# A transformer kernel on one core: late slices normalised on VectorE and split in two places on GpSimd; biases and first queries split on GpSimd in the prelude, and ScalarE issuing part of the first key loads

## The reference

```
x = x + attention_a(norm(x))   # 16 heads of 16; softmax over 2048 keys; the output weighs the row's own v
x = x + ffn(norm(x))           # relu(x Wfc)^2 Wproj, then 5 steps of a spiking neuron, mean spike count
x = x + attention_b(norm(x))   # 16 heads; softmax(k v^T * temperature), applied to q
x = x + ffn(norm(x))
```

## Time and profile before

| what | value |
|---|---|
| three runs, median (lowest to highest) | 2801.47 us (2797.8 to 2804.88) |
| the profiled execution: its time / its span | 2799.21 us / 2797.4 us |
| PE / PEld busy | 2383.7 us (85%) / 1044.3 us (37%) |
| DVE / ACT busy | 2509.2 us (90%) / 2545.7 us (91%) |
| POOL busy | 1301.6 us (47%) |
| L1033 and L1006, DVE maxima, 2048 of them | 1216 and 1219 ns each |
| L1214 and L1257, ACT exp, 2048 of them | 1120 and 1098 ns each |

### The profile page before, as it was taken

One profiled execution on the slowest core, in us unless ns is written; L12 is line 12 of the kernel. 1 busy time (PEld: TensorE's weight loads), 2 busy tenths in 40 slices (PEclk: granted clock), 3 DMA queues, 4 the chain that ended last, 5 costly groups with the idle time before them and its releaser, 6 DMA issues. The chain is left out here.

```text
span 2797.4 us, 43801 instructions
## 1 busy us (share of the span) xinstructions
PE 2383.7 (85%) x12438; PEld 1044.3 (37%) x12672; DVE 2509.2 (90%) x2590; ACT 2545.7 (91%) x4753; POOL 1301.6 (47%) x1913
## 2 busy tenths in 40 slices
PE   5688878877877787777788999999999999999997
PEld 2244444433433443343342333333333333333334
DVE  5898888899999999999988999999999989999994
ACT  2899898999999999999988999999999989999994
POOL 1246666655554554555452244444434434443445
PEclk8999999999999999999999999999999999999999
DMA  6521212143311111111111111111111111111110
GB/s 201 126 63 45 75 44 75 38 100 76 70 35 43 37 35 36 42 30 34 50 36 50 34 45 42 34 40 44 42 31 46 42 29 47 42 37 37 44 28 16
DMA packets 190988, 141.32 MB, mean 51 GB/s; under 512 B 92163, under 2 KB 177669, under 8 KB 190726
## 3 DMA queue, kind: packets, MB, share of 16 engines
q1 hardware_dynamic: 190726, 138.28, 18.6%
HBM read 92.04 MB, written 41.94 MB: 48 GB/s over the span
## 5 line engine op out<-in xcount | busy, mean ns | idle before, releaser
L1033 DVE TENSOR_REDUCE nmax<-score 128x1 f32<-128x1024 f32 x1024 | 1198.2, 1216 | 136.9 <-PE score L814 129.1
L1006 DVE TENSOR_REDUCE nmax<-score 128x1 f32<-128x1024 f32 x1024 | 1211.0, 1219 | 81.2 <-PE score L752 70.1
L1214 ACT ACTIVATE big<-score,nmax 128x1024 f32<-128x1024 f32 x1024 | 1138.4, 1120 | 83.1 <-DVE nmax L1006 77.2
L1257 ACT ACTIVATE score<-score,nmax 128x1024 f32<-128x1024 f32 x1024 | 1118.7, 1098 | 58.2 <-DVE nmax L1033 55.6
L814 PE MATMUL score<-big,shared 128*128 128x512 bf16 x1956 | 627.5, 404 | 250.9 <-ACT score L1257 216.2
L752 PE MATMUL score<-shared 128*128 128x512 bf16 x1906 | 576.6, 385 | 77.5 <-ACT big L1214 48.9
L733 PE MATMUL bank_g<-big,qw 128*32 128x512 f32 x4096 | 547.4, 608 | 1.0 <-ACT qcol L1242 1.0
L752 PEld LDWEIGHTS score<-shared 128*128 128x128 bf16 x2048 | 137.8, 97 | 609.8 <-ACT big L1214 568.3
L814 PEld LDWEIGHTS score<-big,shared 128*128 128x128 bf16 x2048 | 137.1, 99 | 541.9 <-ACT score L1257 449.1
L708 PEld LDWEIGHTS bank_f<-norms,w_fc_sb 128*128 128x128 f32 x2048 | 278.4, 191 | 75.6 <-ACT hid L1179 36.9
L708 PE MATMUL bank_f<-norms,w_fc_sb 128*128 128x128 f32 x2048 | 296.9, 278 | 10.7 <-ACT hid L1179 9.7
(11 more groups left out here) (141 smaller groups left out, 1671.8 us busy)
## 6 DMA issues: line engine op xcount, KB each, us to landing
shared<-q_parts SPq DMA_DIRECT2D x256, 64.0 KB, 2.4
shared<-kb_parts SPq DMA_DIRECT2D x256, 64.0 KB, 2.3
shared<-vb_parts SPq DMA_DIRECT2D x256, 64.0 KB, 2.3
big<-k_parts SPq DMA_DIRECT2D x48, 192.0 KB, 5.0
big<-k_parts SPq DMA_DIRECT2D x24, 256.0 KB, 7.5
kb_parts<-pieces SPq DMA_DIRECT2D x96, 64.0 KB, 1.6
vb_parts<-pieces SPq DMA_DIRECT2D x96, 64.0 KB, 1.6
shared<-in_x SPq DMA_DIRECT2D x32, 128.0 KB, 2.4
```

Source lines behind the costliest of these rows:

```text
L1006: v.tensor_reduce(nmax[:, par, c // NCH, c % NCH:c % NCH + 1], score_b(turn, c)[:, :], AX.X, ALU.max, negate=True).then_inc(max_b, 1)
L1033: v.tensor_reduce(nmax[:, par, c // NCH, c % NCH:c % NCH + 1], score_a(turn, c)[:, :], AX.X, ALU.max, negate=True).then_inc(max_a, 1)
L1214: a.activation(expo[:, c // NCH, (c % NCH) * CH:(c % NCH + 1) * CH], score_b(turn, c)[:, :], ACT.Exp, bias=nmax[:, par, c // NCH, c % NCH: ...
L1257: a.activation(s[:, :], s[:, :], ACT.Exp, bias=nmax[:, par, c // NCH, c % NCH:c % NCH + 1], accum_out=esum[:, par, c // NCH, c % NCH:c % N ...
```

## The change

In the late rows (iterations 3 to 10): `slice_norm` is cut in two. POOL keeps the 1/sqrt(var) (`slice_rstd`), now behind `split_kv`; DVE does the two normalising instructions (`slice_norm`, at c = 25, and slice 0's in the prelude). The slice's statistics move from c = 17, 19 to c = 14, 16. `step_split` is cut in two: `first_part` (cast, subtract) stands before POOL's second `normalise`, `other_parts` (cast, subtract) at the very end of POOL's iteration.

In the prelude: the biases and the queries of group 0 (j = 1) are split by POOL; DVE does its norms first and then splits 0, 2, 3, 4. SP stores in the order j = 0, 2, 1, 3, then issues `load_q(0, 0)`, then stores j = 4. The key loads become seven: heads 0-3 first half, heads 0-1 second half, heads 2-3 second half, then heads 4-5, 6-8, 9-11, 12-15 whole. ScalarE issues the first (8 DMAs) as soon as groups 0 and 1 are stored, and half of the second (4 DMAs) when all are.

```diff
-KEY_LOADS = [(0, 2), (2, 5), (5, 9), (9, 13), (13, 16)]
+KEY_LOADS = [(0, 4, 0, SEQ // 2), (0, 2, SEQ // 2, SEQ), (2, 4, SEQ // 2, SEQ), (4, 6, 0, SEQ), (6, 9, 0, SEQ), (9, 12, 0, SEQ),
+             (12, 16, 0, SEQ)]
+POOL_SPLIT, STORE_ORDER = 1, [0, 2, 1, 3]
...
+        def split_of(j):
+
+            if j == POOL_SPLIT:
+                return q_split, 4
+            return p_split, 4 * (j if j < POOL_SPLIT else j - 1) + 4
...
+            for j in STORE_ORDER:
+                g, m0 = EARLY[j]
+                if j == 2:
+                    sp.wait_ge(bias_split, 4)
+                    for a in range(PARTS):
+                        sp.dma_start(bias[a:a + 1, :], bias_parts[a]).then_inc(bias_loaded, 16)
                 store_group(g, j, k_parts if m0 else q_parts)
...
+            sp.wait_ge(qk_stored[1], 16 * PARTS)
+            load_q(sp, 0, 0)
+            store_group(NE - 1, len(EARLY) - 1, k_parts)
+            for u in range(2):
+                load_slice(u)
             for r in range(2):
                 sp.wait_ge(qk_stored[r], 16 * PARTS * ((len(EARLY) + 1 - r) // 2))
...
+            early_load(1, range(0, 4))
+            early_load(2)
+            store_v(0)
+            early_load(3)
+            early_load(4)
+            load_q(sp, 1, 1)
+            early_load(5)
+            early_load(6)
...
+            def slice_norm(u):
+                dve.wait_ge(s_rstd, 2 * u + 2)
+                need(dve, s_tr, u)
+                dve.wait_ge(s_aggr, SLS * u + SLS)
+                for s in range(SLS):
+                    last = v.tensor_scalar(s_n[:, s, :], s_x[:, u % 2, s, :], s_mv[:, s, 0:1], s_rs[:, s:s + 1],
+                                           ALU.subtract, ALU.mult)
+                last.then_inc(s_xn, 1)
+
             stats(0)
             norm(0)
             stats(1)
             norm(1)
-            split_bias()
             stats(2)
-            split(0)
             norm(2)
-            split(1)
+            scale_bias()
             stats(3)
             norm(3)
+            split(0)
             for j in range(2, len(EARLY)):
                 split(j)
             slice_stats(0)
             slice_aggr(0)
+            slice_norm(0)
...
                     if u is not None and u + 1 < NSL:
-                        if c == 17:
+                        if c == 14:
                             slice_stats(u + 1)
-                        if c == 19:
+                        if c == 16:
                             slice_aggr(u + 1)
+                        if c == 25:
+                            slice_norm(u + 1)
...
+            act.wait_ge(qk_stored[0], 16 * PARTS * 2)
+            load_keys(act, 0, *KEY_LOADS[0], early_keys[0])
             take_v(0)
+            for r in range(2):
+                act.wait_ge(qk_stored[r], 16 * PARTS * ((len(EARLY) + 1 - r) // 2))
+            load_keys(act, 0, *KEY_LOADS[1], early_keys[1], range(4, 8))
...
             for g in range(NE):
                 group_rstd(g)
...
+            split_bias()
+            split_queries(POOL_SPLIT)
...
                 if i2 is not None:
                     spikes(i2, i2, par, 2, 3)
+                if w is not None:
+                    first_part(w)
                 if i1 is not None:
                     normalise(i1, 0, ffn_mv, ffn_step, xn[:, :], xin[:, 1 - par, :], ffn_tr, i1).then_inc(ffn_xn, 1)
-                if w is not None:
-                    step_split(w)
...
                 if i3 is not None:
                     split_kv(i3)
+                if u is not None and u + 1 < NSL:
+                    slice_rstd(u + 1)
...
                     result(i2, i2, par, x2_stored[par], 8 * (i2 - par))
-                if u is not None and u + 1 < NSL:
-                    slice_norm(u + 1)
+                if w is not None:
+                    other_parts(w)
```

More of the change, by code:

```diff
@@ L198, in build @@
         prod = shared2[:, 0:BANK]
+        qres = shared2[:, 0:KC * GROUP].rearrange("p (m n) -> p m n", m=KC)
         qcol = sb("qcol", [P, 2, D])
@@ L299, in stand_alone, with load_q, load_keys @@
                 need(eng, s, n)
+        def split_of(j):
+            if j == POOL_SPLIT:
+                return q_split, 4
+            return p_split, 4 * (j if j < POOL_SPLIT else j - 1) + 4
+        def load_q(eng, i, par):
+            for n in range(8):
+                src = q_parts[Q_SLOTS[n], :, bass.ds(i * P, P)].rearrange("(h d) n -> d h n", d=DH)
+                eng.dma_start(qstack[n:P:8, par, :, :], src).then_inc(q_loaded[par], 16)
+        def load_keys(eng, b, h0, h1, m0, m1, done, copies=range(8)):
+            for n in copies:
+                src = k_parts[K_SLOTS[n], h0 * DH:h1 * DH, b * SEQ + m0:b * SEQ + m1].rearrange("(h d) m -> d h m", d=DH)
+                eng.dma_start(keys[n:P:8, b, h0:h1, m0:m1], src).then_inc(done, 16)
         def tile_at(it, lag):
@@ L429, in store_slice @@
                           .then_inc(s_stored, 16)
[L431 to L439, removed]
             load_x(0)
@@ L515, in phase_a @@
                         stand_alone(sp, (scores_a, CPT * i))
-                        load_q(i + 1, 1 - par)
+                        load_q(sp, i + 1, 1 - par)
                     stand_alone(sp, (att_opt, i - 1), (ffn_x1, i - 1))
@@ L807, in phase_a @@
                     if i is not None:
-                        for n, (h, _) in enumerate(KEY_LOADS):
-                            if isinstance(i, int) and i == 0 and c == h * NCH:
+                        for n, (h, _, m, _) in enumerate(KEY_LOADS):
+                            if isinstance(i, int) and i == 0 and c == h * NCH + m // CH:
                                 pe.wait_ge(early_keys[n], 128)
@@ L905, in split @@
             def split(j):
+                first = split_of(j)[1] - 4
                 dve.wait_ge(p_qkf, j + 1)
@@ L1102, in take @@
             def take(j, m0):
-                need(act, p_split, 4 * (j - 1))
+                if j >= 2:
+                    act.wait_ge(*split_of(j - 2))
                 for m in range(KC):
@@ L1325, in group_rstd, with split_queries, split_bias, slice_rstd @@
                 g_.tensor_tensor(prstd[:, g, :], pvar[:, g, :], power[:, 0:SUB], ALU.pow).then_inc(p_rstd, 1)
+            def split_queries(j):
+                stand_alone(pool, (p_qkf, j + 1))
+                part, whole = pparts[j % 2], pk[j % 2]
+                g_.tensor_scalar(part[:, 0, :, :], whole, 1.0, 0.0, ALU.mult, ALU.add).then_inc(q_split, 1)
+                pool.wait_ge(q_split, 1)
+                g_.tensor_tensor(qres, whole, part[:, 0, :, :], ALU.subtract).then_inc(q_split, 1)
+                stand_alone(pool, (q_split, 2))
+                g_.tensor_scalar(part[:, 1, :, :], qres, 1.0, 0.0, ALU.mult, ALU.add).then_inc(q_split, 1)
+                pool.wait_ge(q_split, 3)
+                g_.tensor_tensor(part[:, 2, :, :], qres, part[:, 1, :, :], ALU.subtract).then_inc(q_split, 1)
+            def split_bias():
+                stand_alone(pool, (w_in_loaded, 16 * N_PRELUDE_LOADS))
+                g_.tensor_scalar(bias_parts[0], row_bias, 1.0, 0.0, ALU.mult, ALU.add).then_inc(bias_split, 1)
+                pool.wait_ge(bias_split, 1)
+                g_.tensor_tensor(bias_res, row_bias, bias_parts[0], ALU.subtract).then_inc(bias_split, 1)
+                stand_alone(pool, (bias_split, 2))
+                g_.tensor_scalar(bias_parts[1], bias_res, 1.0, 0.0, ALU.mult, ALU.add).then_inc(bias_split, 1)
+                pool.wait_ge(bias_split, 3)
+                g_.tensor_tensor(bias_parts[2], bias_res, bias_parts[1], ALU.subtract).then_inc(bias_split, 1)
             for g in range(NE):
                 group_rstd(g)
-            def slice_norm(u):
+            split_bias()
+            split_queries(POOL_SPLIT)
+            def slice_rstd(u):
                 stand_alone(pool, (s_aggr, SLS * u + SLS))
@@ L1334, in slice_norm, with first_part @@
                 g_.tensor_tensor(s_rs, s_var, power[:, 0:SLS], ALU.pow).then_inc(s_rstd, 1)
[L1336 to L1342, removed]
+            def first_part(w):
                 if w < NE - 1:
@@ L1350, in step_split, with other_parts @@
                 g_.tensor_tensor(s_res, s_f, s_parts[:, 0, :, :], ALU.subtract).then_inc(s_split, 1)
+            def other_parts(w):
                 stand_alone(pool, (s_split, 4 * w + 2))
@@ L1354, in step_split @@
                 g_.tensor_tensor(s_parts[:, 2, :, :], s_res, s_parts[:, 1, :, :], ALU.subtract).then_inc(s_split, 1)
-            slice_norm(0)
+            slice_rstd(0)
             def normalise(n, which, got, step, dst, src, free, count):
```

38 lines of the change are left out of this document (9 added, 29 removed).

## The result

The changed kernel takes 2787.53 us (median of 7 runs, 2782.4 to 2793.73), against 2800.08 for the kernel before in 7 runs beside and ahead of it: ratio 0.9957, interval 0.9941 to 0.9972. It is 12.5 us faster. The forecast was 2778, with a range from 2768 to 2787: the sign was right, a little over half of the gain came, and the time lies just above the range. The profiled execution took 2783.98 us (span 2781.9).

The account below looks back on a forecast made before the run. No single engine bounds the kernel; PE's wait for POOL's norm and the prelude were read separately. Slices 24.1 us off, prelude 0.9 lost: 23.2 off 2799.2 gives 2776 profiled, 2778 as median; range 2768 to 2787.

Parts of the forecast that it names:

- the bound of the slice iterations: Iterations 4 to 10: without PE's wait for POOL's L1338, each takes 43.4 us instead of 46.84, 24.1 us off.
- DVE's share: Slice iterations: DVE's added normalising and earlier statistics cost 0.6 us an iteration, bounds 0 and 1.5 us.
- the step that failed: Prelude: only POOL's four subtractions, 2.13 us each, hold up DVE's casts or subtractions; last stores land at 60.8.
- The chain behind split 0: Prelude: splits and stores in turn; without a block split 0 ends at 27.6 and the last stores land at 56.9.
- 62.4 us for the landing: Prelude: where the last stores would land if DVE and POOL blocked each other both ways, by the skill's rule.
- a second term: First tile: ends 53.3 us behind the last stores' landing; at 60.8 that gives 114.1, 0.9 us lost.
- The megabyte that ScalarE loads early: Prelude: ScalarE issues 1 MB of keys at about 41 to 48; the queue takes 5.25 us a MB.
- The new wait that was named: Prelude: SP issues the queries' load, 6.1 us, ahead of the last stores, which wait 3.7 us.
- no block in the prelude: Rival, chance 0.3: POOL's and DVE's prelude instructions pass each other; 27 us off, 2774.
- DVE becomes the bound: Rival, chance 0.13: late norm and denser c = 11 to 16 leave ACT waiting; 44.9 us an iteration, 2789.
- Name changed: Rival, chance 0.04: in the slices PE waits as long for DVE's norm or something behind it; 2799 to 2803.
- POOL's tail: Rival, chance 0.03: `other_parts` at the end of POOL's iteration makes `row_distance` late, stalling ACT, PE, DVE; 2810 and more.

Follow-up runs that it names:

- `norm_at_23`: The changed kernel with the late slices' norm on VectorE at c = 23 instead of c = 25: 2784.87 us, ratio 0.9943.
- experiments 2 and 3: 2: changed kernel with GpSimd's prelude splits given back to VectorE (2776.05 us) or cut short (2778.6 us); 3: kernel before with idle GpSimd operations beside VectorE's splits, only timelines read.
- `small_pool`: The changed kernel with GpSimd's eight prelude operations cut to 2 columns each, the rest set to zero once, results left wrong: 2778.6 us, ratio 0.9923.
- `dve_splits`: The changed kernel with GpSimd's prelude splits (biases, first queries) given back to VectorE behind its norms, stores in order 0, 1, 2, 3: 2776.05 us, ratio 0.9914.
- `recut`: `combined` with the keys cut into other pieces, early DMAs of 128 KB and a last piece of two heads: 2765.78 us, ratio 0.9879.
- `combined`: The changed kernel with the edits of `dve_splits` and `norm_at_23`, and ScalarE issuing the first queries' load: 2770.81 us, ratio 0.9898.

## Why the prediction was wrong

**Right:** the bound of the slice iterations. The wait for L1338 and the half clock behind it are gone; iteration 3 before (43.49 us) was the right model; `first_part` fits POOL's gap; `other_parts` ends 1.93 us ahead of the next work where the prediction had about 1; PE no longer waits for `square`. Marks 4 to 11 lie 306.07 us apart, 43.7 each; forecast was 43.4, with bounds of 42.8 and 44.9. The 0.6 us for DVE's share was too small: the norm took 1.61 instead of 0.75, blocked by `square`, and iteration 10, which has neither norm nor statistics, lasts 42.46 against the others' 43.94, 1.5 us less (the statistics are in these 1.5 us too). With the norm unblocked (`norm_at_23`) they last 43.1, so 0.8 us of it is the block, which the term left out; without it the forecast of 43.4 would have been 0.3 too high. That the mean of 43.7 lies so near is in part because iteration 10 carries none of this. Iterations 4 to 10 gained 21.8 us by chunk 0's exp instead of 24.1, and iteration 3, which the forecast left unchanged, became 0.45 us longer (43.94): together some 2.7 us of the miss.

**Wrong, the step that failed:** "I let each of POOL's four subtractions (2.13 us) hold up a DVE cast or subtraction that comes during it, and its casts not: split 0 then ends at 30.9, split 2 at 39.8, and the last stores land at 60.8". By that step the block costs 3.9 us (a landing at 60.8 instead of 56.9); measured it costs 10.7. It went wrong in three ways, all to be seen in the rows after and in experiments 2 and 3. POOL's casts block too: those of the earlier trace rows that did not were the slow form with pointer scalars (1.23 us for 256 columns), not the (mult, add) that splits. DVE's norm is blocked as well, 5.4 us, which the prediction left out; it counted only DVE's splits. And the block runs both ways, so that the two engines fall into step, one instruction of each at a time. Split 0 ended at 38.0, split 2 at 45.8, and the last stores landed at 67.1. The chain behind split 0 was right: without the block it gives 27.6 for split 0 and 56.9 for the landing, and `small_pool` has 27.3 and 56.4. The Trainium skill, SBUF — State Buffer, "Who interferes with whom", says that the one that comes first blocks the other for its whole instruction, in both directions. The runs bear that out for the fast forms on long operands; for the slow forms of GpSimd they do so only in the direction from VectorE to GpSimd (the pointer form's 2.01 us for 1.22). The prediction's 62.4 us for the landing by this rule was too early as well; its working isn't shown, but the prediction starts split 0 at 23.7, behind a norm that nothing holds up.

**Wrong, a second term:** "the first tile ends at 113.2 now, at landing + 53.3 then". It ends 56.5 us behind the landing (67.13 to 123.67), and in `dve_splits` and `small_pool` 57.3. Of the 3.2 us, 2.6 are the arrival of the last piece (44.6 us behind the landing, at 111.76, instead of 42) and 0.6 the chunks behind it. The megabyte that ScalarE loads early was counted as 5.25 us off the queue; before, the same distance was 57.8, so it brought about 1 us. The prediction took the queue to be full from the landing on; behind the small pieces its share was 0.53 from 70 to 75 us in the changed kernel. `recut`, with the queue full at once and a small last piece, has 52.7 us. The new wait that was named, queries' load ahead of the last stores, is there (57.61 to 62.83, the stores from 62.93), but removing it in `combined` brought next to nothing.

In sum, against the forecast for the profiled execution (2776): the first tile lost 9.2 us more than worked out (10.1 for 0.9), the slices gained 2.7 less, and the untouched part took 4.3 less, which is luck and no part of the change: 7.6 us of the 8 measured (2784). The median of the runs is 9.5 us above its forecast.

**The rivals:** "no block in the prelude" is refuted by the rows; what its time would have been is shown best by `small_pool`, 2778.6 against 2774. "DVE becomes the bound" is partly there: seven iterations last 43.94 us, 0.5 above the forecast's 43.4, where the rival has 44.9. Name changed and POOL's tail did not come.

## What to carry to other kernels

When work moves to an idle engine, ask first what the busy engine's instructions do beside it: 8 us of VectorE's splits given to GpSimd made VectorE finish 13.5 us later than when it did them itself, 10.7 of them by the block. An early transfer is worth only what it takes off a queue that is full afterwards, so cut the pieces that follow so that each issue carries enough, and let the last piece be small and needed late. A neighbour iteration that lacks just one wait is a good price for removing it: here it gave 43.5 us where 43.7 came.

## What was not expected of the hardware

Two instructions of the same name on GpSimd differ by four in speed and in what they do to VectorE: `tensor_scalar` (mult, add) takes 1.04 us for 1024 columns and blocks; (is_gt, add) and the pointer form take 1.07 and 1.23 for 256, and beside them VectorE's instructions were lengthened by 0.2 us or less. The block came with one partition as well: the biases' split on one partition held up a norm over 128 from 1.38 to 6.83 us. And a one-source `tensor_scalar` with pointer scalars on VectorE, which runs no faster than its statistics (411 against about 420 ns for 256 columns), is blocked like the casts (0.41 us each before, up to 2.29 in the changed kernel's fourth norm).
